# Table values of 39 gathered blocks loaded into registers 13 at a time, on TensorE and SyncE

## The reference

```python
shared = silu(x @ shared_gate_w.T) * (x @ shared_up_w.T) @ shared_down_w.T
probs = softmax(x @ router_weight.T)
top_v, top_i = top_k(probs, 2)            # normalised to sum 1
gu = einsum('th,eih->eti', x, gate_up_proj)
gate, up = split(gu, 2)
act = silu(gate) * up
per_expert = einsum('eti,ehi->eth', act, down_proj)
out = einsum('eth,te->th', per_expert, cw) + sigmoid(x @ shared_expert_gate_w.T) * shared
```

## Time and profile before

| | us |
|---|---|
| median of 3 runs | 1028.01 |
| lowest and highest of the runs | 1018.74, 1030.43 |
| span of the profiled execution | 1055.6 |
| TensorE busy in it | 895.3 (85%) |
| VectorE, ScalarE, GpSimd busy | 648.2, 495.7, 551.9 |

### The profile page before, as it was taken

The page is one execution under the profiler, slowest core; times in us unless marked ns, Lnnn a source line. Parts: engine busy times, 40 slices in busy tenths (PEclk is TensorE's granted clock), DMA queues, the critical chain, the costliest instruction groups (busy, mean ns, idle before and its releaser), DMA issues. The chain is left out here.

```text
span 1055.6 us, 18563 instructions
## 1 busy us (share of the span) xinstructions
PE 895.3 (85%) x5465; PEld 753.2 (71%) x5465; DVE 648.2 (61%) x2128; ACT 495.7 (47%) x1781; POOL 551.9 (52%) x634
## 2 busy tenths in 40 slices
PE   4998768999998598888459899999999978999940
PEld 3563447888887488787358799999999966888720
DVE  4603034787787555464258889999999963444441
ACT  1313663444442244454257667877887741222200
POOL 1400122576677135455546866666666653877861
PEclk8978988999999798899779999999999979999985
DMA  9621875589889667986298944514426204899688
GB/s 307 201 94 51 247 209 142 129 250 253 267 237 272 209 209 220 252 300 216 96 227 206 247 122 170 177 65 152 117 66 197 85 14 115 156 222 246 80 201 162
DMA packets 157812, 189.70 MB, mean 180 GB/s; under 512 B 16035, under 2 KB 137017, under 8 KB 157714
## 3 DMA queue, kind: packets, MB, share of 16 engines
q1 hardware_dynamic: 109810, 121.87, 39.9%
q0 software_dynamic: 30720, 46.46, 20.5%
q10 hardware_dynamic: 17184, 20.19, 5.7%
HBM read 96.19 MB, written 103.63 MB: 189 GB/s over the span
## 5 line engine op out<-in xcount | busy, mean ns | idle before, releaser
L1875 POOL DMA_INDIRECT slots_d<-rows,place x128 | 133.4, 1042 | 65.7 <-DVE place L2095 34.5
L1934 ACT ACTIVATE att<-bank,mx 128x77 f32<-128x77 f32 x512 | 160.9, 360 | 1.2 <-DVE mx L2011 1.1
L997 POOL DMA_INDIRECT y_d<-rows x78 | 77.6, 995 | 96.3 <-DVE rows L1375 71.5
L1934 ACT ACTIVATION_READ_ACCUMULATOR att<-bank,mx 128x1 f32 x512 | 123.6, 241 | 0.0
L957 POOL DMA_INDIRECT slots_d<-rows,place x64 | 63.9, 998 | 19.0 <-issue 18.8
L1397 PE MATMUL bank<-wd_hi,act_hi 128*128 128x256 f32 (+1 forms) x206 | 68.5, 332 | 2.7 <-DVE act_lo L1370 1.4
L1889 POOL DMA_INDIRECT acc_d<-expert_out,target_rows x32 | 49.6, 1551 | 26.2 <-issue 25.4
L1399 PE MATMUL bank<-wd_hi,act_lo 128*128 128x256 f32 (+1 forms) x206 | 60.1, 292 | 0.0
L1398 PE MATMUL bank<-wd_lo,act_hi 128*128 128x256 f32 (+1 forms) x206 | 60.0, 291 | 0.0
L2011 DVE TENSOR_REDUCE mx<-bank 128x6 f32<-128x462 f32 (+1 forms) x96 | 55.3, 576 | 5.6 <-PE bank L2195 5.2
L1889 POOL DMA_INDIRECT result<-expert_out,target_rows x32 | 49.5, 1547 | 16.9 <-DMA result<-expert_out,target_rows 8.1
(11 more groups left out here) (322 smaller groups left out, 2998.2 us busy)
## 6 DMA issues: line engine op xcount, KB each, us to landing
rows<-slots_d SPq DMA_DIRECT2D x39, 260.0 KB
slots_d<-zrow SPq DMA_DIRECT2D x8, 1168.0 KB
expert_rows<-slots_d SPq DMA_DIRECT2D x32, 292.0 KB
expert_gate_up<-in_wgu SPq DMA_DIRECT2D x28, 256.0 KB
x_res<-y_d POOLq DMA_DIRECT2D x14, 512.0 KB
wqk_d<-wqk SPq DMA_DIRECT2D x32, 154.0 KB
vwo_d<-vwo SPq DMA_DIRECT2D x16, 308.0 KB
x_res<-in_x SPq DMA_DIRECT2D x8, 512.0 KB
```

The source lines that it names most:

```text
L997: pool.indirect_dma_start(y0_d, bass.IndirectOffsetOnAxis(ap=x_rows(s)[:, b, D:D + 1].bitcast(I32), axis=0), y_rows(s, b), None, bounds_ch ...
L1875: pool.indirect_dma_start(slots_d, bass.IndirectOffsetOnAxis(ap=place[:, n % 3, k:k + 1], axis=0), rows[:, n % 3, :], None, bounds_check=S ...
L1934: last = act.activation(att[:, par, h * S:(h + 1) * S], bank[:, a, i * S:(i + 1) * S], ACT.Exp, scale=-1.0, bias=mx[:, par, h:h + 1], accu ...
```

## The change

SyncE and TensorE no longer load one value per block. At blocks 0, 13 and 26 (`OWNERS = 13`) each loads the 13 values of the coming group with one instruction that fills 13 registers, and checks each of the 13. On SyncE this stands ahead of the wait for a free buffer. On TensorE the first group stands ahead of the transposes of block 0; those of blocks 13 and 26 stand at the head of the round, ahead of the transposes of blocks 15 and 28.

```diff
--- before.py
+++ after.py
@@ -788,6 +788,7 @@
             scat_end = [SCAT[g] + 32 * sum(s // 2 % 6 == g for s in range(BLOCKS)) for g in range(6)]
 
             FIRST_SCORES = BLOCKS - 10
+            OWNERS = 13
             DENSE_PARTS = 2 * (CHUNKS - 1)
 
             def block_part(s, phase):
@@ -897,15 +898,20 @@
                     for i in range(3):
                         sp.wait_ge(moved[i], moved_to[i])
                     sp.wait_ge(cleared, 16 * (2 * (CHUNKS - 1) + 1 + E0))
+                    starts = {}
                     for s in range(BLOCKS + 4):
                         if s >= 4 and block_part(s - 4, 1) is not None:
                             load_part(block_part(s - 4, 1))
                         if s >= BLOCKS:
                             continue
+                        if s % OWNERS == 0:
+                            group = range(s, min(s + OWNERS, BLOCKS))
+                            _, values = nc.values_load_multi_w_load_instructions(
+                                rowtab[0:1, group.start:group.stop], engines=[mybir.EngineType.SP], min_val=0, max_val=PAD0)
+                            starts.update(zip(group, values))
                         if s >= NX:
                             sp.wait_ge(scattered[pair(s)], SCAT[pair(s)] + 64 * (s // NX))
-                        row = sp.value_load(rowtab[0:1, s:s + 1], min_val=0, max_val=PAD0)
-                        sp.dma_start(x_rows(s), slots0_d[bass.ds(row, 2 * P), :].rearrange("(b p) w -> p b w", p=P))\
+                        sp.dma_start(x_rows(s), slots0_d[bass.ds(starts[s], 2 * P), :].rearrange("(b p) w -> p b w", p=P))\
                           .then_inc(in_x[s % NX], 16)
                         if s == BLOCKS // 2 + 2:
                             clear(CHUNKS - 1)
@@ -1496,6 +1502,12 @@
 
                     owners = {}
 
+                    def load_owners(s):
+                        group = range(s, min(s + OWNERS, BLOCKS))
+                        _, values = nc.values_load_multi_w_load_instructions(
+                            owntab[0:1, group.start:group.stop], engines=[mybir.EngineType.PE], min_val=0, max_val=(E0 - 1) * D)
+                        owners.update(zip(group, values))
+
                     def block_rows(s):
                         pe.wait_ge(in_x[s % NX], XIN[s % NX] + 16 * (s // NX + 1))
                         want(pe, ln_xT, XT + s - 1 if s > 1 else 0)
@@ -1506,7 +1518,6 @@
                         last.then_inc(ln_T, 1)
 
                     def block_gate_up(s):
-                        owners[s] = pe.value_load(owntab[0:1, s:s + 1], min_val=0, max_val=(E0 - 1) * D)
                         pe.wait_ge(ln_xT, XT + s + 1)
                         pe.wait_ge(sg_ready, U0 + s - 1)
                         pe.wait_ge(prod_ready, U0 + s - 1)
@@ -1538,11 +1549,14 @@
 
                     pe.wait_ge(table_ready, TABLE + 2)
                     pe.wait_ge(w_lo_ready, 2 + E0)
+                    load_owners(0)
                     block_rows(0)
                     block_rows(1)
                     for s in range(BLOCKS + 2):
                         if s == 2:
                             pe.wait_ge(chunk_added, CHUNKS)
+                        if s and s % OWNERS == 0:
+                            load_owners(s)
                         if s + 2 < BLOCKS:
                             block_rows(s + 2)
                         if s < BLOCKS:
```

## The result

The changed kernel takes 1040.7 us (median of 4 runs, 1034.66 to 1049.21), the kernel before, run beside it, 1026.38 (median of 4, 1018.74 to 1030.43). The ratio is 1.017, with a 95% interval of 1.0118 to 1.0218: slower. On the medians it is 14.3 us (1.4%); the ratio, which is not worked out as the quotient of these two medians, stands for some 17 us, and its interval for 12 to 22. The forecast was 12.5.

A forecast was written before the change was run, and what follows sets the result against it. TensorE, with the least slack in the gathered blocks (365 to about 515 us), was taken to bound the kernel. 4.15 + 6.2 + 4.4 - 2.0 - 0.2 = +12.5 us on 1028.0 gives 1040.5 us, range 1024 to 1052.

The forecast's parts named there:

- The start: At block 0, SyncE's longer load and 12 more pairs delay the first transfer 6.1 us, first gate matmul +4.15 us.
- TensorE's first load hides under SyncE's delay: Ahead of block 0's transposes: TensorE's 6.7 us load ends near 368, costing nothing; without SyncE's part, some 3 us late.
- Block 13: TensorE, ahead of block 15's transposes: sequencer held 6.7 us plus 0.1, lead 0.5 plus 0.1, so 6.2 us exposed.
- I take one read per value: Price of a 13-value load: some 0.23 us per read, so 12 more values add 2.8 us.
- Block 26: TensorE, ahead of block 28's transposes: the lead is 2.3 us plus 0.1, so 4.4 us of the hold is exposed.
- The loads that go: 36 fewer loads on TensorE before gate matmuls: the 2.0 us of idle put down to issue at L1397 goes.
- Clock: TensorE after each of two new pauses: a half-clock stretch costing 1.7 us, together +3.4 us.
- Catching up: ScalarE and VectorE finish owed work during TensorE's two pauses; one average product wait of 1.8 us swallowed each, -3.6 us.
- SyncE at 13 and 26: SyncE's later group loads hold it 6.1 us more, but rows have 10 us of cover; costed at nothing.
- one load, one price: Rival, chance 0.30: 13 values cost what one costs, 2.8 us less at each of three places; +4.1, 1032.1 us.
- Loads under traffic: Rival, chance 0.10: reads at one TensorE place take 1.0 us each, 9.2 more; +21.7, 1049.7 us.
- The load was the path: Rival, chance 0.06: the sequencer sets gate matmul starts, 36 blocks gain 0.37 us each; -7.2, 1020.8 us.

The follow-up runs named there:

- second execution of before: The kernel before, unchanged, run again for a second trace: 1023.83 us (12 runs), ratio 0.9994; the profiled span is 1022.6 us.

## Why the forecast was right, and which terms were not

The direction and the mechanism held: two pauses before the transposes of blocks 15 and 28 put down to issue, and a late first transfer. The total, 12.5 against 14.3 measured, is better than its terms, and that is luck: stops priced 5.4 us too low met waits of the kernel before that were priced too low as well. By the ratio it lies at the lower end of 12 to 22 us.

- *The start, +4.15.* The first transfer was to move by 6.1 us and moved by 5.4 (7.6 to 13.0); the first gate matmul moved by 3.1 (16.2 to 19.3). By block 12 the kernel is 3.8 us late. The size was nearly right for a partly wrong reason: the load of 13 from value 0 is four reads, 0.97 us when nothing runs, and took 2.97 in a stretch with a DMA share of 1.02. That TensorE's first load hides under SyncE's delay held; alone it made the start 2.0 us late, where some 3 was said.
- *Block 13, +6.2.* 7.82 exposed. Hold predicted 6.8, measured 10.0 from the load's start at 401.2 to the transposes at 411.24, of which the array's remaining work covered 2.2 and not 0.6. The failed step is "I take one read per value ... 12 more values add 2.8 us": the reads are one by one as said, but take twice as long as they do in a quiet machine (6.2 us for 13). The lead, read from one load of another execution, was underpriced too, in the other direction.
- *Block 26, +4.4.* 8.19 exposed, for the same reason; the lead of 2.3 + 0.1 was right (10.4 from 446.8 to 457.18, 2.2 of it covered).
- *The loads that go, −2.0.* The second execution of before has 0.7.
- *Clock, +3.4.* The two stretches are there, 3.5 us at 0.52 behind the first stop, and cost 1.6 and 2.4 us (blocks 15 to 16 and 28 to 29 take 4.3 and 5.2 us instead of 2.8). But before has one too, behind its own wait at block 22, worth 2.6, so the net is 1.4. The prediction counted only the new ones.
- *Catching up, −3.6.* In the two traces this is where the underpriced loads were made good. I gave each stop one average wait for the product, 1.8 us; the first one took the place of a 7.0 us wait for rows, and not because ScalarE and VectorE caught up but because block 22's rows were sent for later, clear of the clear. The waits for the product and for act_lo that went are 2.2 us in all. The earlier trace rows have no wait for rows of that size, so the prediction could not read it there, but the trace I had came from one unusually long execution, and I should have kept this term as wide as the waits of the whole stage.
- *SyncE at 13 and 26, nothing.* Held: no wait of TensorE for rows over 0.6 us from 365 us on.

Of the rivals, "one load, one price" fell (3 to 6.6 us a load, not 0.3). "Loads under traffic" was right that the reads stretch, on TensorE by two, but put the cost at 9.2 us for one place where the stops at two places are 5.4 longer than forecast between them (7.82 + 8.19 - 6.2 - 4.4), and did not foresee what the first stop swallows. "The load was the path" fell with the groups of four: 29 of 39 blocks without a load and without a stop, and no gain that can be told.

The Trainium skill ("Runtime: NRT & Kernel Launch", section "Instruction fetch mechanics") has about 200 ns per register, even for bulk loads; it speaks of registers loaded from HBM, where these are loaded from SBUF. SyncE's 2677 ns for 13 values agrees with it (206 each), its 316 ns for four from value 0 does not; for bulk loads that start at a multiple of four the measurement decides. Its floor of about 600 ns for a load ("DMA: Bandwidth & Descriptors", "Latency and other measured facts") is not seen: 272 ns. That unrolling by four pays, which stands beside that floor, is borne out for the price of a load, though not for the time of this kernel.

What stretches TensorE's loads of 13 from 3.1 to 6 us and more is in part open. The array alone does not stretch a load of four: in the kernel with groups of four one ran beside a full array and no transfer, and took 346 ns against 345 with nothing else running (its row, and the window over it):

```profile
L1507 PEldq TENSOR_LOAD <-owner_table x1: 346/346/346, 375.5 to 375.5; - x1
375.50:375.80 0.30, 0.30 (x5) 0.30 (x5) 0.30 (x1) 0.30 (x1) 0.00 (x0) 1.00 0.00 0
```

The long loads all lie in stretches with a DMA share of 1.0, and SyncE's first group takes 2.97 us there against 0.97 with TensorE idle for most of it. That speaks for traffic. But an aligned load of 13 took 2.9 us at a share of 1.00 and 1.1, as in the quiet, at 0.92, so the share alone does not give the size. Open too is why the execution shown before the prediction was 33 us longer than its kin.

## What to carry to other kernels

A load of table values costs nothing as long as the sequencer's lead over its engine covers it. Here that lead was about 2.2 us at both stops and 1.5 to 2.2 at those of the other kernels with groups of 13; a hold of 1.6 us (groups of 4) made no stop. Bunching loads bought nothing, and of a bunch longer than the lead the rest is paid, with a stretch at the lower clock on top. If loads are bunched, four at a time from a multiple of four were the cheapest per value, and the range check of a value (0.28 us) costs no less than its read. Before a wait is priced as swallowed or moved, read a second execution of the same kernel, and do not take what one trace gains for what the runs gain.

## What I had not expected

- Four values from the table's start cost hardly more than one: 316 ns against 272 for one, 472 for two and 864 for four that start at value 2.
- The same load of 13 values took 3.1 us on TensorE in a quiet stretch and 5.2 to 8.8 at work, all from values 13 and 26; SyncE's went from 2.7 only to 3.8.
- A small transfer close behind a large one on the same queue landed late: block 22's rows 18.2 us after issue, behind the clear, where the median of the 39 is 4.0.
- With that clear moved, one execution was 5 us faster and the median of twelve was not.
